# A graph layer on one core: single tiles at the start of the prologue, x in other pieces, the weights' high half on ScalarE

## The chip, the core and the metric

The kernel runs on one core of one Trainium2 chip. The metric is the device time of one execution in microseconds, lower is better. The core has five engines that run their own instruction lists and meet at semaphores: TensorE (PE) for matmuls, VectorE (DVE), ScalarE (ACT), GpSimd (POOL), and the sync engine (SP), which only issues transfers. GpSimd issues transfers too.

## The reference

With N = 2048 nodes and D = 256 features:

```python
h = maximum(layernorm(x), 0)
attn_a = sigmoid(concat([adj @ h, h]) @ Wa.T + ba)      # one gate per node
attn_b = sigmoid(concat([adj @ h, h]) @ Wb.T + bb)
g = h @ W_sa
scores = (g @ a_left)[:, None] + (g @ a_right)[None, :]
e = where(adj != 0, exp(-leaky_relu(scores, 0.01)), 0)
x_a = (e / (sum(e, axis=1) + 1e-5)) @ g
x_b = adj @ (h @ W_gcnb) + b_gcnb
out = x + sigmoid(attn_a * x_a + attn_b * x_b)
```

`adj` is a 2048 x 2048 matrix of zeros and ones. All is fp32; the kernel splits each fp32 operand of a large product into an fp16 high and an fp16 low half (`_hi`, `_lo`) and adds two or three fp16 matmuls.

## The kernel before

The nodes lie in 16 tiles of 128. The output columns of `adj` are taken in four chunks of 512 (`c`). The kernel has a prologue, which works through the 16 tiles of x once, and behind it a long part in which the exponentials of the scores are made and multiplied. The change touches the prologue alone.

The prologue runs over units `u` of two tiles (`NU` = 8). What one unit goes through, with the engine and the line in the kernel before:

- `load_x` (SP, L215): x in five pieces of 2, 2, 4, 4, 4 tiles (`X_PARTS`). The constants `c_sb` and the weights `wa_sb` are issued behind the first piece.
- `moments(u)` (VectorE, L450): for each tile one statistics instruction (L453) and one aggregation of them (L456), and for the unit two small operations (L459, L460) that leave the negated mean and the scaled variance.
- `norms(u)` (GpSimd, L249): the power -0.5 of the variance (L252) and the shift (L254). Between the norms GpSimd issues the pieces of `adj` with `load_adj` (L247), the first when the first piece of x has landed.
- `h0_tiles(u)` (ScalarE, L297): the normalised Relu, in place in `x_sb`, one instruction per tile (L300).
- `turn(u)` (TensorE, L687): transposes of the tile through the identity, two per tile (L693), into bank `u % 2` of PSUM. Unit u waits until unit u - 2 has been read.
- `h0t_highs(u)` (ScalarE, L310) and `h0t_lows(u)` (VectorE, L483): the two fp16 halves of the transposed tiles. Their memory is that of the later `e_hi` and `e_lo`, so the profile names them so.
- `nat_highs(u)` (ScalarE, L306) and `nat_lows(u)` (VectorE, L489): the two halves of the tiles as they are.
- `wide(u)` (TensorE, L704): six matmuls per tile with the weights `wa_hi`, `wa_lo`; 260 columns that hold `g` and four narrow results. Tile t uses one of four banks and waits until tile t - 4 has been read.
- `narrow_results(u)` (VectorE, L494) takes the narrow results out; `mv_highs(u)` (ScalarE, L315 and L319) makes from one of them the exponential scale and the high half of the scaled `g`, one instruction per tile; `mv_lows(u)` (VectorE, L500) the low half.
- `b_products(0, j0, j1)` (TensorE, L730): the aggregation `adj @ h` for chunk 0, four matmuls of 512 columns per tile. It waits for the piece of `adj` and for `nat_lows` of the tile's pair.

No planner sets the order: each engine's list is written out by hand at the end of its block, and each engine goes through its list in that order. In the loop over u, ScalarE does

```python
h0t_highs(u + 1); h0_tiles(u + 2); nat_highs(u + 1); mv_highs(u)
```

and VectorE does

```python
h0t_lows(u + 1); moments(u + 3); narrow_results(u); nat_lows(u + 1); mv_lows(u)
```

so the statistics are three units ahead of the products' halves, and the Relu two. TensorE does `turn(u + 1)`, `wide(u)`, `b_products` of the unit. Before the loop TensorE multiplies zeros (`warm`, L795), nine matmuls (`WARM`) while nothing has landed and six (`WARM_TURN`) between `turn(0)` and `wide(0)`; their results are not used. The product L802 makes four more columns of the wide weights, which VectorE splits in `w_wide` (L463) together with the loaded ones.

Behind the prologue TensorE goes on with `sl_rows`, the aggregation of chunks 1 and 2, and the long products with `e_hi` and `e_lo` (L753 to L755).

Of the kernel before, what the change touches and what calls it, by code (L numbers as in the profile page):

```python
# [67 lines left out]
def build(nc, x, adj_t, w_wide, w_post, consts, rows, out):  # L68
    with ExitStack() as ctx:
# [226 lines left out]
        def _(act):  # L296
            def h0_tiles(u):  # L297
                act.wait_ge(norm_ready, u + 1)
                for t in range(2 * u, 2 * u + 2):
# [8 lines left out]
            def h0t_highs(u):
                act.wait_ge(turned, u + 1)
                act.activation(h0t_hi[:, :, 2 * u * P:(2 * u + 2) * P], turn_bank(u),  # L310
                               ACT.Copy).then_inc(h0t_high, 1)

            def mv_highs(u):
                act.wait_ge(exs_ready, u + 1)
                act.activation(scale_a[:, 2 * u:2 * u + 2], exs[:, 2 * u:2 * u + 2, SR], ACT.Exp, bias=log_s[:, 0:1],  # L315
                               scale=-SLOPE).then_inc(scales_ready, 1)
# [543 lines left out]
```

## Time and profile before

| | us |
|---|---|
| three timed executions | 182.90, 182.56, 182.02 |
| their median | 182.56 |
| the profiled execution | 182.3 |
| its span in the profile | 180.5 |

| engine | busy us | share of the span |
|---|---|---|
| TensorE | 175.3 | 97% |
| VectorE | 146.5 | 81% |
| ScalarE | 115.8 | 64% |
| GpSimd | 17.8 | 10% |

The span is the time from the first to the last instruction; the execution has 1.8 us around it. A high share says which engine has much to do, not when it waits. Where an engine begins to be fed, and by whom, is read from the chain of waits and from the timelines of the first 40 us, which hold the prologue. Starts are in microseconds from the start of the span. Where a row merges several instructions (x2, x9), its length runs from the start of the first to the end of the last; instructions overlap a little at their ends, so the next one of the same engine can start before the one ahead has ended.

### The profile page before, as it was taken

What the parts mean: (1) busy time and instruction counts of PE and PEld (TensorE: products, weight loads), DVE (VectorE), ACT (ScalarE), POOL (GpSimd) and SP (SyncE); (2) the same over time, 40 slices, a digit from 0 to 9 for tenths busy, and PEclk for the clock granted to TensorE, in tenths of its full rate; (3) what the DMA queues carried; (4) which work ended last, traced back from release to release, by engine and by line L of the source; (5) the groups of instructions that cost most, each with busy time, mean ns of one, the idle gap of its engine ahead of it and who ended that gap; (6) DMA issues with size and microseconds to landing.
All of it is one profiled execution on the core that took longest, in us unless ns stands there. A gap on an engine that the chain in (4) does not pass through costs nothing.

```text
span 180.5 us, 3416 instructions
## 1 busy us (share of the span) xinstructions
PE 175.3 (97%) x1335; PEld 128.7 (71%) x1335; DVE 146.5 (81%) x306; ACT 115.8 (64%) x170; POOL 17.8 (10%) x39
## 2 busy tenths in 40 slices
PE   7899999999999999999999999999999999999993
PEld 2656776664544448888864468888888888888892
DVE  1759989748899999599999920999999999987542
ACT  3358788963999987748395640494785686673410
POOL 2544364230000200000000000000000000000000
PEclk9999999999999999999999999999999999999999
DMA  5998967899980598000001100000010010011101
GB/s 172 303 298 143 189 102 162 154 220 241 244 310 5 87 205 172 0 4 0 2 4 58 58 0 4 0 0 0 4 58 0 4 60 0 4 60 56 64 29 29
DMA packets 4767, 15.81 MB, mean 88 GB/s; under 512 B 528, under 2 KB 1040, under 8 KB 3856
## 3 DMA queue, kind: packets, MB, share of 16 engines
q0 software_dynamic: 1440, 8.39, 24.3%
q1 hardware_dynamic: 3312, 7.22, 11.3%
q8 instruction: 10, 0.16, 0.4%
q14 instruction: 5, 0.04, 0.1%
HBM read 21.90 MB, written 2.10 MB: 133 GB/s over the span
## 4 chain that ended last, share of the span: by engine, by line
PE 91%; DMA 7%; DVE 0%; issue 0%; ACT 0%; DVEq 0%
PE ps L730 31%; PE ps L754 16%; PE ps L755 16%; PE ps L753 16%; PE ps L746 6%; PE ps L704 5%; DMA adj<-in_adj_t 5%; DMA x_sb<-in_x 2%; PE ps L693 2%; PE ps L715 1%; DVE logit L673 0%; ACT logit L370 0%; DVE res L589 0%; DVEq L672 0%
## 5 line engine op out<-in xcount | busy, mean ns | idle before, releaser
L753 PE MATMUL ps<-mv_lo,e_hi 128*128 128x257 f16 (+2 forms) x272 | 71.0, 267 | 0.0
L755 PE MATMUL ps<-mv_hi,e_lo 128*128 128x257 f16 (+2 forms) x272 | 70.9, 266 | 0.0
L754 PE MATMUL ps<-mv_hi,e_hi 128*128 128x257 f16 (+2 forms) x272 | 70.8, 266 | 0.0
L336 ACT ACTIVATE z<-z,log_e 128x1024 f32<-128x1024 f32 x32 | 36.7, 1147 | 29.0 <-DVE z L526 29.0
L730 PE MATMUL ps<-adj,nat_hi 128*128 128x512 f16 x128 | 48.5, 379 | 0.2 <-DMA adj<-in_adj_t 0.2
L730 PE MATMUL ps<-adj,nat_lo 128*128 128x512 f16 x128 | 48.5, 379 | 0.0
L526 DVE SCALAR_TENSOR_TENSOR z<-sl_row,exs,far 128x512 f32<-128x512 f32 x64 | 45.1, 746 | 0.0
L534 DVE TENSOR_TENSOR e_lo<-z,e_hi 128x1024 f16<-128x1024 f32 x32 | 39.0, 1219 | 1.3 <-ACT e_hi L346 1.3
L346 ACT ACTIVATE e_hi<-z 128x1024 f16<-128x1024 f32 x32 | 33.3, 1041 | 0.0
L754 PEld LDWEIGHTS ps<-mv_hi,e_hi 128*128 128x128 f16 x272 | 26.5, 98 | 3.2
L753 PEld LDWEIGHTS ps<-mv_lo,e_hi 128*128 128x128 f16 x272 | 26.4, 97 | 3.3
L755 PEld LDWEIGHTS ps<-mv_hi,e_lo 128*128 128x128 f16 x272 | 26.4, 97 | 3.1
L730 PEld LDWEIGHTS ps<-adj,nat_hi 128*128 128x128 f16 x128 | 12.5, 98 | 14.6 <-DMA adj<-in_adj_t 0.5
L730 PEld LDWEIGHTS ps<-adj,nat_lo 128*128 128x128 f16 x128 | 12.5, 98 | 13.9
L515 DVE TENSOR_SCALAR far<-adj 128x1024 f16<-128x1024 f16 x32 | 13.3, 420 | 0.2
L300 ACT ACTIVATE x_sb<-x_sb,shift,rstd 128x256 f32<-128x256 f32 x16 | 8.7, 599 | 4.4 <-POOL shift L254 4.4
L370 ACT ACTIVATE logit<-logit 128x512 f32<-128x512 f32 (+2 forms) x10 | 5.4, 536 | 9.3 <-DVE logit L576 5.3
L543 DVE SCALAR_TENSOR_TENSOR gate_in<-ps,gate_c 128x4 f32<-128x4 f32 x8 | 1.3, 159 | 10.6 <-PE ps L746 10.6
L252 POOL TENSOR_TENSOR rstd<-var_s,power 128x2 f32<-128x2 f32 x8 | 8.1, 1013 | 13.6 <-DVE var_s L460 13.6
L500 DVE SCALAR_TENSOR_TENSOR mv_lo<-ps,scale_a,mv_hi 128x256 f16<-128x256 f32 x16 | 7.0, 480 | 2.5 <-ACT mv_hi L319 2.5
L704 PE MATMUL ps<-wa_hi,e_hi 128*128 128x260 f16 x32 | 8.8, 275 | 0.0
L746 PE MATMUL ps<-wg_hi,agg_hi 128*128 128x258 f16 x32 | 8.8, 274 | 0.0
(69 smaller groups left out, 184.8 us busy)
## 6 DMA issues: line engine op xcount, KB each, us to landing
adj<-in_adj_t POOLq DMA_DIRECT2D x7, 1024.0 KB, 9.7
x_sb<-in_x SPq DMA_DIRECT2D x7, 512.0 KB, 11.4
out<-res SPq DMA_DIRECT2D x7, 256.0 KB, 2.0
x_sb<-in_x SPq DMA_DIRECT2D x2, 256.0 KB, 4.1
adj<-in_adj_t POOLq DMA_DIRECT2D x2, 256.0 KB, 7.1
adj<-in_adj_t POOLq DMA_DIRECT2D x1, 512.0 KB, 5.7
c_sb<-in_consts SPq DMA_DIRECT2D x1, 258.0 KB, 3.5
wa_sb<-in_w_wide SPq DMA_DIRECT2D x1, 258.0 KB, 3.7
```

The lines of the kernel that those rows point to most:

```text
L300: act.activation(x_sb[:, t, :], x_sb[:, t, :], ACT.Relu, bias=shift[:, t:t + 1], scale=rstd[:, t:t + 1]).then_inc(h0_done, 1)
L336: act.activation(z[:, n % ZRING, :, :], z[:, n % ZRING, :, :], ACT.Exp, bias=log_e[:, 0:1], scale=SLOPE - 1.0).then_inc(exp_done, 1)
L346: act.activation(e_hi[:, s:s + 2, :], z[:, n % ZRING, :, :], ACT.Copy).then_inc(e_high, 1)
L515: dve.tensor_scalar(far[:, n % 2, :, :], adj16[:, c % ADJ, j:j + 2, :], -FAR, FAR, ALU.mult, ALU.add)\
L526: ins = dve.scalar_tensor_tensor(out=z[:, n % ZRING, u, :], in0=sl_row[:, c * CW:(c + 1) * CW], scalar=exs[:, j + u, SR:SR + 1], in1=far[: ...
L534: dve.tensor_tensor(e_lo[:, s:s + 2, :], z[:, n % ZRING, :, :], e_hi[:, s:s + 2, :], ALU.subtract)\
L704: ins = pe.matmul(ps[:, WIDE_BANKS[u % 2] + t % 2, 0:WA], h0t[a][:, k, t * P:(t + 1) * P], wa2[b][:, k, :], start=(i == 0), stop=(i == len ...
L730: ins = pe.matmul(ps[:, B_BANKS[c] + k, :], nat[h][:, j, k * P:(k + 1) * P], adj16[:, c % ADJ, j, :], start=(j == 0 and h == 0), stop=(j = ...
L746: ins = pe.matmul(ps[:, 6 + q, 0:WG], agg[a][:, c % AGG, k, cols], wg2[b][:, k, :], start=(i == 0), stop=(i == len(three) - 1))
L753: pe.matmul(ps[:, bank, cols], e_hi[:, s, i1], mv_lo[:, j, cols], start=(j == 0), stop=False)
L754: pe.matmul(ps[:, bank, cols], e_hi[:, s, i1], mv_hi[:, j, cols], start=False, stop=False)
L755: return pe.matmul(ps[:, bank, cols], e_lo[:, s, i1], mv_hi[:, j, cols], start=False, stop=(j == NT - 1))
```

## The change

Units get sizes of their own (`UNITS`): the first four hold one tile each, the other six two tiles, so that `NU` is 10 and the loop begins at unit 4 (`U0`). The Relu, the transposes, the transposed halves, `wide` and the statistics go by units; the natural halves, the narrow results and the scaled `g` still go by pairs of tiles `p`. For unit u of the loop its pair is u - 2. The orders ahead of the loops are written out anew on VectorE, ScalarE and TensorE. x comes in pieces of 1, 1, 2, 4, 4, 4 tiles, the first two ahead of the constants and the weights; SP waits for the piece with tiles 4 to 7 before it issues the last two and what follows them. The high half of the loaded wide weights is made by ScalarE ahead of its first Relu instead of VectorE. `WARM_TURN` is 2 instead of 6. On GpSimd the pieces of `adj` stand between other norms.

The diff without the renaming of u to p in the halves, the narrow results and `mv_highs`, `mv_lows`:

```diff
--- before.py
+++ after.py
@@ -48,17 +48,19 @@
 R_BAB, R_BIAS = 0, 2
 R_END = R_BIAS + D
 
-NU = NT // 2
 WARM = 9
-WARM_TURN = 6
-X_PARTS = ((0, 2), (2, 4), (4, 8), (8, 12), (12, 16))
+WARM_TURN = 2
+UNITS = ((0, 1), (1, 2), (2, 3), (3, 4), (4, 6), (6, 8), (8, 10), (10, 12), (12, 14), (14, 16))
+NU = len(UNITS)
+U0 = 4
+X_PARTS = ((0, 1), (1, 2), (2, 4), (4, 8), (8, 12), (12, 16))
 WIDE_BANKS = (2, 6)
 B_BANKS = (4, 6, 4, 4)
 ADJ_PIECES = ((0, 0, 2), (0, 2, 4), (0, 4, 8), (0, 8, 16), (1, 0, 8), (1, 8, 16), (2, 0, 8), (2, 8, 16), (3, 0, 8), (3, 8, 16))
 
 
 def x_part(u):
-    return next(i for i, (lo, hi) in enumerate(X_PARTS) if lo <= 2 * u < hi)
+    return next(i for i, (lo, hi) in enumerate(X_PARTS) if lo <= UNITS[u][0] < hi)
 
 
 def piece_of(c, j):
@@ -206,7 +209,14 @@
         last_banks = (3, 1)
 
         def turn_bank(u):
-            return ps[:, u % 2, :].rearrange("p (k n) -> p k n", k=KT)
+            n = (UNITS[u][1] - UNITS[u][0]) * P
+            return ps[:, u % 2, 0:KT * n].rearrange("p (k n) -> p k n", k=KT)
+
+        def h0t_cols(tile, u):
+            return tile[:, :, UNITS[u][0] * P:UNITS[u][1] * P]
+
+        def wide_bank(t):
+            return WIDE_BANKS[t // 2 % 2] + t % 2
 
         block = ctx.enter_context(nc.Block())
 
@@ -217,15 +227,18 @@
                 sp.dma_start(x_sb[:, lo:hi, :], x[:, lo:hi, :]).then_inc(x_landed[i], 16)
 
             load_x(0)
+            load_x(1)
             sp.dma_start(c_sb[:, :], consts).then_inc(c_landed, 16)
             sp.dma_start(wa_sb[:, :, :], w_wide).then_inc(wa_landed, 16)
-            load_x(1)
-            for i in range(2, len(X_PARTS)):
-                load_x(i)
+            load_x(2)
+            load_x(3)
+            sp.wait_ge(x_landed[3], 16)
+            load_x(4)
+            load_x(5)
             sp.dma_start(wg_sb[:, :, :], w_post).then_inc(wg_landed, 16)
             sp.dma_start(r_sb[:, :], rows).then_inc(rows_landed, 16)
             sp.wait_ge(turned, NU)
-            sp.wait_ge(nat_ready, NU)
+            sp.wait_ge(nat_ready, NPAIR)
             for g in range(NG):
                 ts = slice(g * GT, (g + 1) * GT)
                 sp.dma_start(x_sb[:, ts, :], x[:, ts, :]).then_inc(x_back[g], 16)
@@ -247,9 +260,9 @@
                 pool.dma_start(adj16[:, c % ADJ, lo:hi, :], adj_t[c, :, lo:hi, :]).then_inc(adj_landed[i], 16)
 
             def norms(u):
-                ts = slice(2 * u, 2 * u + 2)
+                ts = slice(*UNITS[u])
                 pool.wait_ge(var_ready, u + 1)
-                pool.tensor_tensor(rstd[:, ts], var_s[:, ts], power[:, :], ALU.pow).then_inc(rstd_ready, 1)
+                pool.tensor_tensor(rstd[:, ts], var_s[:, ts], power[:, 0:UNITS[u][1] - UNITS[u][0]], ALU.pow).then_inc(rstd_ready, 1)
                 pool.wait_ge(rstd_ready, u + 1)
                 pool.tensor_tensor(shift[:, ts], neg_mean[:, ts], rstd[:, ts], ALU.mult).then_inc(norm_ready, 1)
 
@@ -264,18 +277,20 @@
             norms(1)
             load_adj(1)
             norms(2)
+            norms(3)
             load_adj(2)
-            norms(3)
-            load_adj(3)
             norms(4)
             norms(5)
-            load_adj(4)
+            load_adj(3)
             norms(6)
             norms(7)
+            load_adj(4)
+            norms(8)
+            norms(9)
             load_adj(5)
             load_adj(6)
             load_adj(7)
-            pool.wait_ge(scales_ready, NU)
+            pool.wait_ge(scales_ready, NPAIR)
             pool.tensor_scalar(column[:, :], scale_a[:, :], PROD, None, ALU.mult).then_inc(column_done, 1)
             pool.wait_ge(column_done, 1)
             pool.tensor_copy(mv_hi[:, :, D], column[:, :]).then_inc(column_high, 1)
...
@@ -371,18 +385,32 @@
 
             act.wait_ge(consts_ready, 1)
             act.activation(table[:, :], log_e[:, :], ACT.Exp)
+            act.wait_ge(wa_landed, 16)
+            act.activation(wa_hi[:, :, 0:WG], wa_sb[:, :, :], ACT.Copy, scale=W_SCALE).then_inc(wa_high, 1)
             h0_tiles(0)
             h0t_highs(0)
+            h0_tiles(1)
+            h0t_highs(1)
             nat_highs(0)
-            h0_tiles(1)
-            for u in range(NU):
+            h0_tiles(2)
+            h0t_highs(2)
+            h0_tiles(3)
+            h0t_highs(3)
+            h0_tiles(4)
+            mv_highs(0)
+            nat_highs(1)
+            h0t_highs(4)
+            h0_tiles(5)
+            mv_highs(1)
+            nat_highs(2)
+            for u in range(U0, NU):
                 if u + 1 < NU:
                     h0t_highs(u + 1)
                 if u + 2 < NU:
                     h0_tiles(u + 2)
                 if u + 1 < NU:
-                    nat_highs(u + 1)
-                mv_highs(u)
+                    nat_highs(u - 1)
+                mv_highs(u - 2)
             act.activation(factor_l[:, :], exs[:, :, SL], ACT.Exp, scale=SLOPE).then_inc(factors_done, 1)
             sl_rows(0)
             sl_rows(1)
@@ -448,27 +476,25 @@
             dve.memset(log_s[:, :], math.log(MV_SCALE / PROD)).then_inc(consts_ready, 1)
 
             def moments(u):
+                lo, hi = UNITS[u]
                 dve.wait_ge(x_landed[x_part(u)], 16)
-                for t in range(2 * u, 2 * u + 2):
+                for t in range(lo, hi):
                     dve.bn_stats(stats[:, t, :], x_sb[:, t, :]).then_inc(stats_done, 1)
-                for t in range(2 * u, 2 * u + 2):
+                for t in range(lo, hi):
                     dve.wait_ge(stats_done, t + 1)
                     dve.bn_aggr(mean_var[:, t, :], stats[:, t, :]).then_inc(moments_done, 1)
-                ts = slice(2 * u, 2 * u + 2)
-                dve.wait_ge(moments_done, 2 * u + 2)
-                dve.tensor_scalar(neg_mean[:, ts], mean_var[:, ts, 0], -1.0, None, ALU.mult)
-                dve.tensor_scalar(var_s[:, ts], mean_var[:, ts, 1], LN_EPS, H_SCALE ** -2, ALU.add, ALU.mult)\
+                dve.wait_ge(moments_done, hi)
+                dve.tensor_scalar(neg_mean[:, lo:hi], mean_var[:, lo:hi, 0], -1.0, None, ALU.mult)
+                dve.tensor_scalar(var_s[:, lo:hi], mean_var[:, lo:hi, 1], LN_EPS, H_SCALE ** -2, ALU.add, ALU.mult)\
                     .then_inc(var_ready, 1)
 
-            def w_wide():
-                dve.wait_ge(wa_landed, 16)
-                dve.tensor_scalar(wa_hi[:, :, 0:WG], wa_sb[:, :, :], W_SCALE, None, ALU.mult).then_inc(wa_high, 1)
+            def w_wide_low():
                 dve.wait_ge(wa_high, 1)
                 dve.scalar_tensor_tensor(out=wa_lo[:, :, 0:WG], in0=wa_sb[:, :, :], scalar=W_SCALE, in1=wa_hi[:, :, 0:WG],
                                          op0=ALU.mult, op1=ALU.subtract)
                 dve.wait_ge(wl_product, 1)
-                dve.tensor_scalar(wa_hi[:, :, WG:WA], wl_bank, W_SCALE, None, ALU.mult).then_inc(wa_high, 1)
-                dve.wait_ge(wa_high, 2)
+                dve.tensor_scalar(wa_hi[:, :, WG:WA], wl_bank, W_SCALE, None, ALU.mult).then_inc(wl_high, 1)
+                dve.wait_ge(wl_high, 1)
                 dve.scalar_tensor_tensor(out=wa_lo[:, :, WG:WA], in0=wl_bank, scalar=W_SCALE, in1=wa_hi[:, :, WG:WA],
                                          op0=ALU.mult, op1=ALU.subtract).then_inc(wa_ready, 1)
 
...
@@ -594,20 +618,34 @@
                 logits(p, p)
 
             moments(0)
-            w_wide()
             moments(1)
+            w_wide_low()
             h0t_lows(0)
+            moments(2)
+            h0t_lows(1)
             nat_lows(0)
-            moments(2)
-            for u in range(NU):
+            moments(3)
+            h0t_lows(2)
+            moments(4)
+            narrow_results(0)
+            h0t_lows(3)
+            mv_lows(0)
+            moments(5)
+            nat_lows(1)
+            narrow_results(1)
+            h0t_lows(4)
+            mv_lows(1)
+            moments(6)
+            nat_lows(2)
+            for u in range(U0, NU):
                 if u + 1 < NU:
                     h0t_lows(u + 1)
                 if u + 3 < NU:
                     moments(u + 3)
-                narrow_results(u)
+                narrow_results(u - 2)
                 if u + 1 < NU:
-                    nat_lows(u + 1)
-                mv_lows(u)
+                    nat_lows(u - 1)
+                mv_lows(u - 2)
             w_post_low()
             dve_far(0)
             for n in range(NE):
@@ -687,21 +725,22 @@
             def turn(u):
                 if u >= 2:
                     pe.wait_ge(h0t_ready, u - 1)
-                for t in range(2 * u, 2 * u + 2):
+                for t in range(*UNITS[u]):
                     pe.wait_ge(h0_done, t + 1)
                     for k in range(KT):
-                        ins = pe.transpose(turn_bank(u)[:, k, t % 2 * P:(t % 2 + 1) * P], x_sb[:, t, k * P:(k + 1) * P], ident[:, :])
+                        cols = slice((t - UNITS[u][0]) * P, (t - UNITS[u][0] + 1) * P)
+                        ins = pe.transpose(turn_bank(u)[:, k, cols], x_sb[:, t, k * P:(k + 1) * P], ident[:, :])
                 ins.then_inc(turned, 1)
 
             def wide(u):
                 pe.wait_ge(h0t_ready, u + 1)
                 if u == 0:
                     pe.wait_ge(wa_ready, 1)
-                for t in range(2 * u, 2 * u + 2):
-                    if u >= 2:
+                for t in range(*UNITS[u]):
+                    if t >= 4:
                         pe.wait_ge(mv_ready, t - 3)
                     for i, (k, a, b) in enumerate(three):
-                        ins = pe.matmul(ps[:, WIDE_BANKS[u % 2] + t % 2, 0:WA], h0t[a][:, k, t * P:(t + 1) * P],
+                        ins = pe.matmul(ps[:, wide_bank(t), 0:WA], h0t[a][:, k, t * P:(t + 1) * P],
                                         wa2[b][:, k, :], start=(i == 0), stop=(i == len(three) - 1))
                     ins.then_inc(wide_product, 1)
 
@@ -805,14 +844,22 @@
             pe.wait_ge(ident_ready, 3)
             turn(0)
             warm(WARM_TURN)
+            turn(1)
             wide(0)
-            turn(1)
-            b_products(0, 0, 2)
-            for u in range(1, NU):
+            wide(1)
+            b_products(0, 0, 1)
+            turn(2)
+            b_products(0, 1, 2)
+            wide(2)
+            turn(3)
+            turn(4)
+            wide(3)
+            b_products(0, 2, 4)
+            for u in range(U0, NU):
                 if u + 1 < NU:
                     turn(u + 1)
                 wide(u)
-                b_products(0, 2 * u, 2 * u + 2)
+                b_products(0, *UNITS[u])
             sl_rows(0)
             sl_rows(1)
             b_products(1, 0, 8)
```

## Rows read from the trace of the kernel before

**Rows 1.** The page: busy time of the engines, and the granted clock in 40 slices.

```profile
PE 175.3 (97%) x1335; PEld 128.7 (71%) x1335; DVE 146.5 (81%) x306; ACT 115.8 (64%) x170; POOL 17.8 (10%) x39
...
PEclk9999999999999999999999999999999999999999
```

**Rows 2.** The chain that ended last, 0 to 60 us: start, length, what.

```profile
4.30 8.48 DMA adj<-in_adj_t
...
18.66 1.33 PE ps L704 x12
20.00 1.73 PE ps L730 x8
21.72 0.44 PE ps L693 x4
```

**Rows 3.** Timeline of TensorE: start, length in us, instruction, [idle before it].

```profile
1.18 4.02 PE L795 MATMUL ps<-e_hi 128*128 128x512 f16 x9 [1.18 <-DVE e_hi L446]
...
7.39 1.09 PE L693 MATMUL ps<-ident,x_sb 128*128 128x128 f32 x4 [0.69 <-ACT x_sb L300]
8.27 2.55 PE L795 MATMUL ps<-e_hi 128*128 128x512 f16 x6
10.66 0.27 PE L704 MATMUL ps<-wa_hi,e_hi 128*128 128x260 f16 x1
```

**Rows 4.** Timeline of VectorE.

```profile
4.03 0.75 DVE L453 BATCH_NORM_STATS2 stats<-x_sb 128x6 f32<-128x256 f32 x2 [2.89 <-DMA x_sb<-in_x]
...
13.26 0.69 DVE L483 TENSOR_TENSOR e_lo<-ps,e_hi 128x512 f16<-128x512 f32 x1 [1.68 <-ACT e_hi L310]
13.87 0.74 DVE L453 BATCH_NORM_STATS2 stats<-x_sb 128x6 f32<-128x256 f32 x2
...
17.50 0.74 DVE L453 BATCH_NORM_STATS2 stats<-x_sb 128x6 f32<-128x256 f32 x2
...
18.71 0.68 DVE L489 TENSOR_TENSOR nat_lo<-x_sb,nat_hi 128x512 f16<-128x512 f32 x1
19.67 0.88 DVE L500 SCALAR_TENSOR_TENSOR mv_lo<-ps,scale_a,mv_hi 128x256 f16<-128x256 f32 x2 [0.28 <-ACT mv_hi L319]
20.52 0.69 DVE L483 TENSOR_TENSOR e_lo<-ps,e_hi 128x512 f16<-128x512 f32 x1
```

**Rows 5.** Timeline of ScalarE.

```profile
6.64 1.09 ACT L300 ACTIVATE x_sb<-x_sb,shift,rstd 128x256 f32<-128x256 f32 x2 [4.43 <-POOL shift L254]
8.51 0.60 ACT L310 ACTIVATE e_hi<-ps 128x512 f16<-128x512 f32 x1 [0.78 <-PE ps L693]
...
18.83 0.30 ACT L315 ACTIVATE scale_a<-exs,log_s 128x2 f32<-128x2 f32 x1 [0.48 <-DVE exs L494]
19.16 0.84 ACT L319 ACTIVATE mv_hi<-ps,scale_a 128x256 f16<-128x256 f32 x2
...
20.37 1.09 ACT L300 ACTIVATE x_sb<-x_sb,shift,rstd 128x256 f32<-128x256 f32 x2
21.35 0.63 ACT L306 ACTIVATE nat_hi<-x_sb 128x512 f16<-128x512 f32 x1
```

**Rows 6.** Timeline of GpSimd.

```profile
4.30 0.71 POOL L247 DMA_DIRECT2D adj<-in_adj_t  x1 [2.81 <-DMA x_sb<-in_x]
...
8.33 0.70 POOL L252 TENSOR_TENSOR rstd<-var_s,power 128x2 f32<-128x2 f32 x1 [1.72 <-DVE var_s L460]
...
18.82 1.15 POOL L252 TENSOR_TENSOR rstd<-var_s,power 128x2 f32<-128x2 f32 x1 [1.66 <-DVE var_s L460]
20.05 0.20 POOL L254 TENSOR_TENSOR shift<-neg_mean,rstd 128x2 f32<-128x2 f32 x1
```

**Rows 7.** Timeline of the sync queue.

```profile
1.63 0.42 SPq L221 DMA_DIRECT2D wa_sb<-in_w_wide  x1
```

**Rows 8.** DMA issues by kind: KB each, us from issue to landing.

```profile
wa_sb<-in_w_wide SPq DMA_DIRECT2D x1, 258.0 KB, 3.7
...
out<-res SPq DMA_DIRECT2D x1, 128.0 KB, 1.8
```

More of the change, by code:

```diff
@@ L150, in build @@
         wa_high = sem("wa_high")
+        wl_high = sem("wl_high")
         wa_ready = sem("wa_ready")
@@ L298, in h0_tiles, with nat_highs, mv_highs @@
                 act.wait_ge(norm_ready, u + 1)
-                for t in range(2 * u, 2 * u + 2):
+                for t in range(*UNITS[u]):
                     act.activation(x_sb[:, t, :], x_sb[:, t, :], ACT.Relu, bias=shift[:, t:t + 1],
                                    scale=rstd[:, t:t + 1]).then_inc(h0_done, 1)
-            def nat_highs(u):
-                ts = slice(2 * u, 2 * u + 2)
-                act.wait_ge(h0_done, 2 * u + 2)
-                act.activation(nat_hi[:, ts, :], x_sb[:, ts, :], ACT.Copy).then_inc(nat_high, 1)
             def h0t_highs(u):
                 act.wait_ge(turned, u + 1)
[L310 to L315, printed above, removed]
+                act.activation(h0t_cols(h0t_hi, u), turn_bank(u), ACT.Copy).then_inc(h0t_high, 1)
+            def nat_highs(p):
+                ts = slice(2 * p, 2 * p + 2)
+                act.wait_ge(h0_done, 2 * p + 2)
+                act.activation(nat_hi[:, ts, :], x_sb[:, ts, :], ACT.Copy).then_inc(nat_high, 1)
+            def mv_highs(p):
+                act.wait_ge(exs_ready, p + 1)
+                act.activation(scale_a[:, 2 * p:2 * p + 2], exs[:, 2 * p:2 * p + 2, SR], ACT.Exp, bias=log_s[:, 0:1],
                                scale=-SLOPE).then_inc(scales_ready, 1)
-                act.wait_ge(scales_ready, u + 1)
-                for t in range(2 * u, 2 * u + 2):
-                    act.activation(mv_hi[:, t, 0:D], ps[:, WIDE_BANKS[u % 2] + t % 2, 0:D], ACT.Copy,
+                act.wait_ge(scales_ready, p + 1)
+                for t in range(2 * p, 2 * p + 2):
+                    act.activation(mv_hi[:, t, 0:D], ps[:, wide_bank(t), 0:D], ACT.Copy,
                                    scale=scale_a[:, t:t + 1]).then_inc(mv_high, 1)
@@ L481, in h0t_lows, with nat_lows, narrow_results, mv_lows @@
                 dve.wait_ge(h0t_high, u + 1)
-                cols = slice(2 * u * P, (2 * u + 2) * P)
-                dve.tensor_tensor(h0t_lo[:, :, cols], turn_bank(u), h0t_hi[:, :, cols],
-                                  ALU.subtract).then_inc(h0t_ready, 1)
-            def nat_lows(u):
-                ts = slice(2 * u, 2 * u + 2)
-                dve.wait_ge(nat_high, u + 1)
+                dve.tensor_tensor(h0t_cols(h0t_lo, u), turn_bank(u), h0t_cols(h0t_hi, u), ALU.subtract).then_inc(h0t_ready, 1)
+            def nat_lows(p):
+                ts = slice(2 * p, 2 * p + 2)
+                dve.wait_ge(nat_high, p + 1)
                 dve.tensor_tensor(nat_lo[:, ts, :], x_sb[:, ts, :], nat_hi[:, ts, :], ALU.subtract).then_inc(nat_ready, 1)
-            def narrow_results(u):
-                bank = WIDE_BANKS[u % 2]
-                dve.wait_ge(wide_product, 2 * u + 2)
-                dve.tensor_scalar(exs[:, 2 * u:2 * u + 2, :], ps[:, bank:bank + 2, D:D + NX], 1.0 / PROD, None, ALU.mult)\
+            def narrow_results(p):
+                bank = wide_bank(2 * p)
+                dve.wait_ge(wide_product, 2 * p + 2)
+                dve.tensor_scalar(exs[:, 2 * p:2 * p + 2, :], ps[:, bank:bank + 2, D:D + NX], 1.0 / PROD, None, ALU.mult)\
                     .then_inc(exs_ready, 1)
-            def mv_lows(u):
-                for t in range(2 * u, 2 * u + 2):
+            def mv_lows(p):
+                for t in range(2 * p, 2 * p + 2):
                     dve.wait_ge(mv_high, t + 1)
-                    dve.scalar_tensor_tensor(out=mv_lo[:, t, 0:D], in0=ps[:, WIDE_BANKS[u % 2] + t % 2, 0:D],
+                    dve.scalar_tensor_tensor(out=mv_lo[:, t, 0:D], in0=ps[:, wide_bank(t), 0:D],
                                              scalar=scale_a[:, t:t + 1], in1=mv_hi[:, t, 0:D],
```

4 lines of the change are left out of this document (1 added, 3 removed).

## The prediction

> **What bounds the kernel now.** I read the page first: TensorE is busy 97% of the span, and the page's clock line says full speed everywhere [rows 1]. Then the chain of waits for the first 60 us [rows 2]. Its first long piece is the transfer of the first adjacency piece, which lands at 4.30 + 8.48 = 12.78 us. From there on it is matmuls without a gap: for each pair of tiles 1.33 us of wide projection, 1.73 us of aggregation and 0.44 us of transposes, 3.50 us in all. So the end moves with two things only: when TensorE begins its useful work, and whether it stays fed after that. Third, TensorE's timeline before 11 us [rows 3]: nine matmuls on zeros from 1.18 us, transposes from 7.39 us, six matmuls on zeros from 8.27 us, and the first wide matmul at 10.66 us. Nine 512-column matmuls in 4.02 us, the last one 0.6 us long, start 0.43 us apart; the chain has the same size 1.73/8 = 0.216 us apart at 20 us. So the engine was at its lower level (1.2 GHz) here although the page's clock line shows full speed, and it rose to the upper one (2.4 GHz) shortly before 10.66 us, after some 3 us in which it worked without a pause from 7.39 us.
>
> Last, the timelines of the three engines that feed it [rows 4 to 6]. They are not far from being the bound themselves. VectorE starts the same step (`moments`) at 13.87 and at 17.50 us: a period of 3.63 us against TensorE's 3.50. The cover that makes it work is lookahead: in the loop over units VectorE does `moments(u+3)`, ScalarE `h0_tiles(u+2)`, so that the way from `moments` over GpSimd's `norms` to ScalarE's `h0_tiles` is hidden by a whole pair's work. Each engine takes its instructions in order: at 11.58 us VectorE had all it needed for `moments(3)` (tiles 6 and 7 are in the same x piece as tiles 4 and 5, on which it had just worked), but sat idle 1.68 us until 13.26, because `h0t_lows(1)` stood ahead of it; `moments(3)` began at 13.87 [rows 4].
>
> **The change part by part.**
>
> *x in smaller pieces.* The first piece shrinks from 256 to 128 KB. It now lands at 4.03 [rows 4]; a lone 128 KB transfer takes 1.8 us [rows 8], so the new landing lies between 0.72 + 1.8 = 2.5 and 4.0 us; I take 3.4, a bit nearer to the measured one as others still follow at its heels. `moments(0)` on one tile: statistics 0.41 and the rest as before, about 0.9 us, so done at 4.3 instead of 5.3.
>
> *GpSimd.* `load_adj(0)` moves up with x; the issue is 0.71 us [rows 6] and the power then follows at about 4.4, and `norms(0)` is done at 5.7, `norms(1)` at about 7.
>
> *ScalarE makes the weights' high half first.* The weights land at 1.63 + 3.7 = 5.3 us [rows 7, 8] and are issued one DMA (0.42 us) later now: 5.6. The conversion is like the 512-column `nat_highs`, 0.63 us [rows 5], with 0.51 until the next starts: `h0_tiles(0)` at 6.15 instead of 6.64. It is queued behind the weights, and that eats half of the microsecond just won. VectorE loses the 0.46 us of `wa_hi`.
>
> *Single tiles.* Now ScalarE alternates `h0_tiles` and `h0t_highs` for one tile each. From the end of a Relu to the high half of its transposes it waits 0.78 us (7.73 to 8.51) [rows 5]. A step is 0.49 (half of the pair, 21.35 - 20.37, rows 5) + 0.1 + 0.78 + 0.3 (half of 0.60), near 1.65 us for each of tiles 0 and 1, none of it hidden: tile 0's high half starts at 7.6, tile 1's at 9.3, `nat_highs(0)` at 9.6. VectorE's `nat_lows(0)` follows at 10.3 and is done at 11.0.
>
> *Fewer matmuls on zeros.* Four go, 4 x 0.43 = 1.7 us at the lower level. That removes them from the way to `wide(0)`, which can begin at 9.0, when `h0t_lows(0)` and `turn(1)` are through; so far a gain of 10.66 - 9.0 = 1.7 us. But the engine is then still at its lower level, where a wide tile takes 6 x 0.217 = 1.3 us instead of 0.66: `wide(0)` and `wide(1)` end at 11.2 to 11.6, the aggregation of tile 0 takes 0.86 (upper) to 1.7 us (lower), and `turn(2)` comes behind it: 12.0 to 12.8. The adjacency piece is issued 0.6 us earlier with fewer transfers ahead; bounds from 4.3 to 12.8 us, I take 10.5, not on the path. `h0t_highs(2)` is at 12.4 to 13.2, `h0t_lows(2)` on VectorE at 12.9 to 13.6.
>
> *The new order on VectorE and ScalarE.* Here is the cost. VectorE's list runs: `h0t_lows(2)`, `moments(4)`, `narrow_results(0)`, `h0t_lows(3)`, `mv_lows(0)`, `moments(5)`, `nat_lows(1)`, ..., `mv_lows(1)`, `moments(6)`, `nat_lows(2)`. ScalarE's: `h0_tiles(4)`, `mv_highs(0)`, ..., `h0_tiles(5)`, `mv_highs(1)`. So `mv_lows(0)` waits for `mv_highs(0)`, that is queued behind `h0_tiles(4)`, that needs `moments(4)`; and `moments(5)` is queued behind `mv_lows(0)`. The lookahead is gone: the next pair's statistics begin only when the last pair's whole round has come back. One round, all from rows:
> - `moments` start to power start: 18.82 - 17.50 = 1.32 [rows 4, 6];
> - power start to ScalarE's start: 20.25 - 18.82 = 1.43, + 0.03 = 1.46 [rows 6]; 1.0 if the power is the 0.70 one (it is that short while VectorE is idle, 8.33 us);
> - two Relus: 0.98 [rows 5];
> - the exponential's start to the start of `mv_lows`: 19.67 - 18.83 = 0.84 [rows 4, 5];
> - both `mv_lows`: 20.52 - 19.67 = 0.85 [rows 4].
>
> Sum 5.45 us (5.0 with short powers) where a pair took 3.63. Twice: `moments(4)` starts 0.35 us after `h0t_lows(2)`, at 13.25 to 13.95. `mv_lows(0)` ends 5.45 later, 18.7 to 19.4; `moments(5)` starts there, `mv_lows(1)` ends 24.15 to 24.85; `moments(6)` takes 1.14, and `nat_lows(2)` starts at 25.3 to 26.0 and is done 0.68 later [rows 4], 26.0 to 26.7. TensorE needs it for the aggregation of tiles 4 and 5, which stands on the chain at 20.00 [rows 2]. New: 26.1 to 26.8, middle 26.5. It comes 6.5 us later.
>
> Beyond that point the loop has the old lookahead, TensorE has the same work left in the same order, and nothing of it can be given back, since it runs gapless behind this point and the exponential stage begins on VectorE after the same loop. TensorE's own work up to there is done with waits, so the clock costs little more. The hidden rest: `c_sb` 0.43 us later (its products are small and needed at 9), SP's wait before the last x pieces (tiles 8 on are wanted at 24 us by `moments(6)`, and would be there by 15), the later adjacency pieces (issued behind norms that move with the rest).
>
> Profiled execution: 182.3 = span 180.5 + 1.8 around; + 6.5 gives 188.8. The timed median is 182.56, 0.26 above the profiled one: 189.0.
>
> The Trainium skill, TensorE: Matmul & The Clock Gate, Part 1, says that the array's normal state is throttled and that only activity releases it; the page's advice is not to leave TensorE idle between bursts. The trace shows the release [rows 3], and no fall, as TensorE never pauses afterwards. It is the ground for the second rival.
>
> **The rivals.**
>
> 1. *The start counts and the round is hidden: faster.* Place: TensorE's start. From `turn(1)` at 8.65 it would have 7 x 0.22 of transposes, 6 x 0.665 of wide and 4 x 0.865 of aggregation = 9.0 us until the chain's 20.00, + 1.5 for three microseconds at the lower level: 19.2, 0.8 earlier, 1.5 if the clock rises sooner: 181.4. For it: the first tile is ready sooner, the zeros are gone. Against it: this needs `nat_lows(2)` done by 20.0, and the two rounds would have to take (19.9 - 0.7 - 1.1 - 13.6)/2 = 2.2 us each, where the rows give 5.45. It decides only if the order on the two queues doesn't bind as I read it. 9%.
>
> 2. *The clock falls in the new gaps.* With the rounds, TensorE has some 2.4 us idle before tiles 4 and 5 are turned, as much before the aggregation of tile 2, and about 1.8 before that of tile 4. If it drops to the lower level there, the work behind 26.5 us runs at half speed until it rises again; before, that took 3 us [rows 3], which would cost 1.5 us, more if it comes late: 190.5 to 191.5. For it: it began low and needed work to rise. Against: half of the time it works. 14%.
>
> 3. *Only one round is exposed.* If short powers and quick halves let ScalarE reach `mv_highs(0)` without waiting, one round is as before: 6.5 - 1.8 = 4.7 or, with short powers too, 3.8: 186.4 to 187.3. Against: nothing stands between `moments(4)` and `h0_tiles(4)` that could hide the way. 8%.
>
> 4. *No change*, if late parts have slack that I missed: 3%.
>
> **How the numbers follow.** The forecast (two open rounds) has 66%: 189.0, its own range 187.5 to 190.3 from short powers (-1.0) and the clock rising at 14 instead of 12 us (+0.8). The range reaches into rivals 2 and 3: 186.6 to 191.0. About 0.5% is what a measurement of this kernel can tell from no change. Faster 9%, same 3%, slower 88%.
>
> **What would show it.** In the changed kernel's trace: VectorE idle some 2 us or more before each `mv_lo` of tiles 0 and 2, waiting for ScalarE; ScalarE idle about 2.5 us before the Relu of tiles 6 and 8, waiting for GpSimd's `shift`; the starts of the statistics of tiles 4, 6 and 8 over 5 us apart, then 3.6; aggregation of tiles 4 and 5 near 26 us; first wide matmul near 9 us with 0.22 us between starts. It is wrong if the statistics keep 3.6 us apart from tile 4 on, or if TensorE shows no gaps between 14 and 26 us.

## The result and the profile after

The changed kernel takes 188.74 us (median of four executions, 188.16 to 189.25), the kernel before 182.73 us measured with them. The ratio is 1.0326, 95% interval 1.028 to 1.0371: 6.0 us slower. The profiled execution took 189.25 us, the longest of the four, with a span of 187.4 us: 6.9 more than before. Here and below the ratios leave out executions that are more than 1.5% above the shortest one of their kernel; medians and ranges hold all of them.

The page of the changed kernel, busy time and granted clock:

```profile
PE 177.2 (95%) x1331; PEld 128.8 (69%) x1331; DVE 147.1 (78%) x311; ACT 116.9 (62%) x173; POOL 18.5 (10%) x43
...
PEclk9969579999999999999999999999999999999998
```

TensorE is busy 1.9 us longer for fewer matmuls, and its clock, full in all slices before [rows 1], now is down to 0.5 in places. By stretches of 2 us (busy time and number of PE, PEld, DVE, ACT, POOL, then clock, DMA share, GB/s):

```profile
10.00:12.00 2.00, 2.00 (x11) 1.32 (x9) 1.67 (x6) 0.91 (x2) 0.43 (x3) 0.50 0.89 227
...
18.00:20.00 2.00, 0.69 (x7) 0.37 (x4) 1.74 (x6) 1.60 (x4) 0.00 (x0) 0.80 0.13 25
20.00:22.00 2.00, 0.97 (x3) 0.43 (x4) 1.52 (x6) 0.26 (x1) 1.56 (x3) 0.50 0.01 4
```

A clock of 0.50 is the lower level, 1.2 GHz. The first such stretch is the start. The kernel before is at its lower level at the start too, by the spacing of its matmuls [rows 3], although its clock line reads full. The second is a fall that the kernel before does not have, within 18 to 20 us; TensorE's timeline shows the pauses around it.

```profile
9.16 0.42 PE L743 MATMUL ps<-wa_hi,e_hi 128*128 128x260 f16 x1
9.37 0.43 PE L743 MATMUL ps<-wa_lo,e_hi 128*128 128x260 f16 x1
...
17.19 0.84 PE L732 MATMUL ps<-ident,x_sb 128*128 128x128 f32 x4 [1.89 <-ACT x_sb L315]
17.86 0.27 PE L743 MATMUL ps<-wa_hi,e_hi 128*128 128x260 f16 x1
17.97 0.27 PE L743 MATMUL ps<-wa_lo,e_hi 128*128 128x260 f16 x1
...
21.03 0.58 PE L769 MATMUL ps<-adj,nat_hi 128*128 128x512 f16 x1 [2.33 <-DVE nat_lo L513]
21.41 0.63 PE L769 MATMUL ps<-adj,nat_lo 128*128 128x512 f16 x1
...
26.96 0.38 PE L769 MATMUL ps<-adj,nat_hi 128*128 128x512 f16 x1
```

The first wide matmul starts at 9.16 us (10.66 before, rows 3), the second 0.21 us later: lower level. A pause of 1.89 us follows; behind it the wide matmuls are still 0.11 us apart, the upper level. Then a pause of 2.33 us, and behind that 512-column matmuls of 0.63 us, 0.42 us apart: the lower level. The Trainium skill (TensorE: Matmul & The Clock Gate, Part 1) has an idle engine go back to the lower level. The trace agrees as far as that: the granted clock is 0.80 over 18 to 20 us, in which the second pause begins, and 0.50 from 20 us on. The aggregation of tiles 4 and 5 starts at 26.96. The chain of waits:

```profile
2.10 4.03 DMA wa_sb<-in_w_wide
...
16.45 1.09 ACT x_sb L315 x2
...
18.26 0.88 DVE mv_lo L524 x2
...
21.03 3.57 PE ps L769 x8
24.60 0.85 PE ps L732 x4
25.45 1.67 PE ps L743 x12
27.12 1.73 PE ps L769 x8
```

Before, the chain was matmuls alone from 12.8 us [rows 2]; now it goes through Relus, `mv_lo` and statistics. And from 21.03 to 27.12 us it is TensorE's own work for tiles 2 and 3, their followers' transposes and the wide tiles 4 and 5: 6.1 us of what took 3.5 (1.73 + 0.44 + 1.33, rows 2). The piece of 1.73 us on tiles 4 and 5, the landmark for what follows, is at 27.12 instead of 20.00: 7.1 us later. (The chain gives a piece from the end of the one ahead of it, so it can stand 0.16 us behind the start in the timeline.) The feeding engines, VectorE first, then ScalarE:

```profile
14.10 0.74 DVE L482 BATCH_NORM_STATS2 stats<-x_sb 128x6 f32<-128x256 f32 x2
...
18.26 0.88 DVE L524 SCALAR_TENSOR_TENSOR mv_lo<-ps,scale_a,mv_hi 128x256 f16<-128x256 f32 x2 [2.08 <-ACT mv_hi L333]
19.05 0.74 DVE L482 BATCH_NORM_STATS2 stats<-x_sb 128x6 f32<-128x256 f32 x2
...
23.56 0.88 DVE L524 SCALAR_TENSOR_TENSOR mv_lo<-ps,scale_a,mv_hi 128x256 f16<-128x256 f32 x2 [2.00 <-ACT mv_hi L333]
24.35 0.74 DVE L482 BATCH_NORM_STATS2 stats<-x_sb 128x6 f32<-128x256 f32 x2
...
25.49 0.68 DVE L513 TENSOR_TENSOR nat_lo<-x_sb,nat_hi 128x512 f16<-128x512 f32 x1
```

```profile
16.45 1.09 ACT L315 ACTIVATE x_sb<-x_sb,shift,rstd 128x256 f32<-128x256 f32 x2 [0.72 <-POOL shift L267]
...
21.74 1.09 ACT L315 ACTIVATE x_sb<-x_sb,shift,rstd 128x256 f32<-128x256 f32 x2 [2.14 <-POOL shift L267]
```

Statistics start at 14.10, 19.05 and 24.35 us: rounds of 4.95 and 5.30 us where the kernel before has 3.63 [rows 4]. Ahead of each `mv_lo` VectorE is idle 2 us for ScalarE, which was idle 2.14 us for the shift of tiles 6 and 7. `nat_lo` of tiles 4 and 5 is done at 25.49 + 0.68 = 26.2 us, 0.8 us before TensorE reaches them. So two limits lie side by side there: the open rounds (26.2) and TensorE's own work at the lower level (27.0). They are not independent: the pause in which the clock fell, and the start of that work at 21.03, are themselves waits for the first open round.

### The profile page after: what moved, and what is told of

It is laid out like the page before. It is cut to its first block, busy times and chain, and to the rows that moved or that the text cites. A ratio compares the mean times of both kernels' runs of the same rounds, so it can differ in the third digit from the quotient of the medians.

```text
span 187.4 us, 3423 instructions
## 1 busy us (share of the span) xinstructions
PE 177.2 (95%) x1331; PEld 128.8 (69%) x1331; DVE 147.1 (78%) x311; ACT 116.9 (62%) x173; POOL 18.5 (10%) x43
## 4 chain that ended last, share of the span: by engine, by line
PE 90%; DVE 3%; ACT 2%; DMA 2%; SPq 1%; issue 1%; POOL 0%; DVEq 0%
PE ps L769 30%; PE ps L794 15%; PE ps L793 15%; PE ps L792 15%; PE ps L743 6%; PE ps L785 6%; DMA wa_sb<-in_w_wide 2%; PE ps L732 2%; ACT x_sb L315 1%; PE ps L754 1%; DVE stats L482 1%; DVE mv_lo L524 0%; SPq L227 0%; ACT e_hi L320 0%; POOL rstd L265 0%
## 5 line engine op out<-in xcount | busy, mean ns | idle before, releaser
L769 PE MATMUL ps<-adj,nat_hi 128*128 128x512 f16 x128 | 49.7, 388 | 2.3 <-DVE nat_lo L513 2.3
L769 PE MATMUL ps<-adj,nat_lo 128*128 128x512 f16 x128 | 49.6, 388 | 0.0
L769 PEld LDWEIGHTS ps<-adj,nat_hi 128*128 128x128 f16 x128 | 12.8, 100 | 17.1 <-issue 3.7
L265 POOL TENSOR_TENSOR rstd<-var_s,power 128x2 f32<-128x2 f32 (+1 forms) x10 | 8.1, 809 | 19.5 <-DVE var_s L488 19.4
L743 PE MATMUL ps<-wa_hi,e_hi 128*128 128x260 f16 x32 | 9.6, 300 | 0.1
L743 PE MATMUL ps<-wa_hi,e_lo 128*128 128x260 f16 x32 | 9.5, 297 | 0.0
```

Source lines behind the costliest of these rows:

```text
L743: ins = pe.matmul(ps[:, wide_bank(t), 0:WA], h0t[a][:, k, t * P:(t + 1) * P], wa2[b][:, k, :], start=(i == 0), stop=(i == len(three) - 1))
L769: ins = pe.matmul(ps[:, B_BANKS[c] + k, :], nat[h][:, j, k * P:(k + 1) * P], adj16[:, c % ADJ, j, :], start=(j == 0 and h == 0), stop=(j = ...
```

## The experiments

**stats_ahead.** The changed kernel, with the statistics one place ahead on VectorE:

```diff
             moments(3)
+            moments(4)
             h0t_lows(2)
-            moments(4)
+            moments(5)
             narrow_results(0)
             h0t_lows(3)
             mv_lows(0)
-            moments(5)
+            moments(6)
             nat_lows(1)
             narrow_results(1)
             h0t_lows(4)
             mv_lows(1)
-            moments(6)
             nat_lows(2)
```

> The changed kernel with one edit on VectorE: moments(4), moments(5) and moments(6) each move one place ahead, in front of h0t_lows(2), narrow_results(0) and nat_lows(1), so that the statistics of a pair no longer wait for mv_lows of the pair before. ScalarE's and TensorE's lists stay. Theory (the open rounds cost the time): the Relus of tiles 6 and 8 no longer wait over 1 us for GpSimd, the starts of mv_lo of tiles 0 and 2 are under 4 us apart instead of 5.3, and some 3 of the 6 to 7 us come back: 185.5, 184.8 to 186.5. What is left is the late start of tiles 2 and 3, whose nat_lows(1) still stands behind moments(6) and mv_highs(0). Rival (single tiles and fewer matmuls on zeros cost it, the order doesn't matter): 188 to 189, as the changed kernel.

Measured: 187.16 us, 185.58 to 188.69; over the three shorter ones of the four the ratio is 1.0225 (1.0167 to 1.0282). The rounds closed; VectorE and then the chain of the profiled execution, which is the longest of the four and not among those three:

```profile
17.28 0.88 DVE L524 SCALAR_TENSOR_TENSOR mv_lo<-ps,scale_a,mv_hi 128x256 f16<-128x256 f32 x2 [1.25 <-ACT mv_hi L333]
...
20.84 0.88 DVE L524 SCALAR_TENSOR_TENSOR mv_lo<-ps,scale_a,mv_hi 128x256 f16<-128x256 f32 x2 [0.27 <-ACT mv_hi L333]
```

```profile
20.05 3.57 PE ps L769 x8
23.62 0.85 PE ps L732 x4
24.47 2.10 PE ps L743 x12
26.57 1.73 PE ps L769 x8
```

`mv_lo` of tiles 0 and 2 are 3.56 us apart (5.30 in the changed kernel), as expected. Of the expected 3.2 us 1.8 came back (by the ratios). In the profiled execution TensorE's own work from tiles 2 and 3 to tiles 4 and 5 takes 6.5 us, nearly all of it at the lower level, and it alone binds. My expectation had no term for the clock, and that was wrong there. The other three are 0.9 to 3.1 us shorter, with a mean granted clock of 0.991 against 0.971; no trace shows what binds them.

**zeros_in_gaps.** The changed kernel, TensorE kept busy:

```diff
             turn(3)
+            spare(7, 8)
             turn(4)
             wide(3)
+            spare(1, 10)
             b_products(0, 2, 4)
```

`spare(bank, n)` multiplies zeros, n matmuls of 512 columns, into a free bank; for bank 1 it first waits until the transposes there have been read.

> The changed kernel with matmuls on zeros in TensorE's two gaps: 8 of 512 columns between turn(3) and turn(4), 10 between wide(3) and the aggregation of tiles 2 and 3, into banks that nobody reads then. Theory (the clock fell in the gaps and cost TensorE the last 0.8 us): the spacing of the 512-column matmuls on tiles 2 and 3 is 0.22 us instead of 0.43, and the aggregation of tiles 4 and 5 then waits for nat_lows(2) alone, at 26.2 instead of 26.96 us: 0.8 us faster than the changed kernel, 187.9 against 188.7. Rival (the clock cost much more than the waits, so that the open rounds explain only part): 3 us or more faster. Second rival (the clock had no effect on the end): no change, within 0.3 us.

Measured: 188.18 us, ratio 1.0303 (1.0268 to 1.0339); by time alone not told apart from the changed kernel. The chain says what binds:

```profile
25.09 0.60 DVE nat_lo L513
...
25.83 1.89 PE ps L769 x8
```

The granted clock is 1.00 from 12 us on, and TensorE waits for `nat_lo` of tiles 4 and 5, which starts at 25.09: the other limit, as expected. It starts on tiles 4 and 5 at 25.83, 1.1 us ahead of the changed kernel's 26.96. Of this 0.4 us is not the edit's: the weights landed at 5.64 us here (6.13 in the changed kernel), and `nat_lo` too started 0.4 us earlier. The 0.7 us left are the 0.8 that I expected.

**ahead_and_zeros.** Both edits (4 and 10 zeros).

> Both edits at once: the statistics of tiles 4 to 9 one place ahead on VectorE (as in stats_ahead) and matmuls on zeros in TensorE's gaps (4 and 10). Each alone gave little: with the statistics ahead the profiled execution had TensorE at its lower level from 19 to 25.8 us, so that tiles 2 and 3 to tiles 4 and 5 took 6.4 us of its own work instead of 3.5; with zeros alone it waited for nat_lows(2) until 25.8 us. Theory (two limits side by side, the open round on VectorE and ScalarE, and TensorE's clock behind the gaps): together they bring the aggregation of tiles 4 and 5 from 26.96 to about 20.05 + 3.5 = 23.6 us: 3.4 us off the changed kernel, 185.3 (184.7 to 185.9), with less spread than stats_ahead alone. Rival (the effects only add up): 188.7 - 1.6 - 0.6 = 186.5 or more.

Measured: 185.5 us, 184.98 to 186.92, ratio 1.0168 (1.0127 to 1.0209).

```profile
18.46 0.60 DVE nat_lo L513
...
19.20 1.89 PE ps L769 x8
...
22.86 1.73 PE ps L769 x8
```

Tiles 4 and 5 at 22.86 us. By their ratios, times 182.6 us, the four kernels stand at +6.0 (neither edit), +5.5 (zeros), +4.1 (statistics ahead) and +3.1 us (both) over the kernel before. So the pair takes back 2.9 us where the single edits add up to 2.3, which the intervals do not tell from a sum: the times do not decide between my theory and its rival. In the chains the landmark is at 27.12, 25.83, 26.57 and 22.86, 4.3 us for the pair against 1.8 for the single edits. But these are one execution each, for neither edit and for the statistics alone the longest of its kernel, for the pair the shortest. That there are two limits is read from the chains, each with one of them binding; how much they overlap in a usual execution is not shown. What is left is the late start of tiles 2 and 3: their `nat_lo` at 18.46, behind `mv_lows(0)` and `moments(6)`.

**before_one_late.** The kernel before, one line moved:

```diff
             nat_lows(0)
-            moments(2)
             for u in range(NU):
                 if u + 1 < NU:
                     h0t_lows(u + 1)
+                if u == 0:
+                    moments(2)
```

> The kernel before with one edit on VectorE: moments(2) no longer stands ahead of the loop but behind h0t_lows(1), right before moments(3). No single tiles, no new pieces of x, all the matmuls on zeros. Theory: this alone opens one round, from the statistics of tiles 4 and 5 over GpSimd to the Relu, that mv_highs(0) stands behind. In the kernel before the statistics start at 10.35 us; now at 13.9, the Relu at 16.6 instead of 13.12, mv_lows(0) at about 18.9 instead of 16.04. VectorE and ScalarE come 2.9 us later, of which TensorE's cover at the end of the prologue takes 0.3: 2.6 us slower, 185.2; up to 186.2 if the clock falls in the new gap. Rival (lookahead is worth little, since TensorE has other work): within 0.7 us of the kernel before.

Measured: 186.53 us (186.43 to 186.71), ratio 1.0223 (1.0201 to 1.0245): 3.9 us for one line, with none of the change's other parts. ScalarE, then the chain:

```profile
16.25 1.09 ACT L300 ACTIVATE x_sb<-x_sb,shift,rstd 128x256 f32<-128x256 f32 x2 [2.98 <-POOL shift L254]
```

```profile
18.08 2.60 PE ps L705 x12
...
24.31 1.73 PE ps L731 x8
```

The exposed way is there (2.98 us idle for the shift), and the wide tiles 2 and 3 took 2.60 us instead of 1.33. I had 2.6 us, or 3.6 with a fall of the clock; it fell, and 3.9 is a little above both.

**one_late_and_zeros.** The same with `warm(9)` in the gap, behind the aggregation of tiles 0 and 1.

> The kernel before with moments(2) behind h0t_lows(1) (as in before_one_late, 3.9 us slower than before) and nine matmuls on zeros behind the aggregation of tiles 0 and 1, in the 2 us gap that this opens. Theory: 2.6 us of the 3.9 are the exposed way from the statistics to the Relu, 1.3 us are the wide projection of tiles 2 and 3 at the lower level; with the clock kept up, 185.3. Rival (the gap itself is the price, the clock adds nothing): 186.5, no change against before_one_late.

Measured: 185.05 us (184.32 to 185.15), ratio 1.012 (1.0081 to 1.0159).

```profile
14.99 1.94 PE ps L796 x9
...
17.37 1.33 PE ps L705 x12
18.70 1.73 PE ps L731 x8
```

The wide tiles take 1.33 us again. What is left over the kernel before, 2.2 to 2.5 us (by the ratio, by the medians), is the exposed round; the 1.5 to 1.9 us that went were the clock.

**relu_first.** The changed kernel, ScalarE's first two steps swapped:

```diff
+            h0_tiles(0)
             act.wait_ge(wa_landed, 16)
             act.activation(wa_hi[:, :, 0:WG], wa_sb[:, :, :], ACT.Copy, scale=W_SCALE).then_inc(wa_high, 1)
-            h0_tiles(0)
```

> The changed kernel with one edit on ScalarE: the Relu of tile 0 stands ahead of the high half of the weights. Theory (the chain of the changed kernel begins with the transfer of the weights, which ScalarE waits for until 6.15 us while the shift of tile 0 is there at 5.28): the first Relu at 5.3, tile 0's transposes done before the weights are split, its high half at 6.7 instead of 7.87, about 0.6 to 1.1 us earlier for all that follows until the adjacency piece or the norms bind: 187.9, 0.8 faster. Rival (the gain is lost at norms(2) or at the first adjacency piece): no change.

Measured: 188.54 us, ratio 1.0327 (1.0274 to 1.0379): no change, the rival.

```profile
3.47 7.89 DMA adj<-in_adj_t
...
20.38 3.57 PE ps L769 x8
...
26.72 1.73 PE ps L769 x8
```

The chain now begins with the first adjacency piece, which lands at 11.36 us; of the 0.8 us 0.4 arrive at tiles 4 and 5, too little to measure.

**before_two_zeros.** The kernel before with `WARM_TURN = 2`.

> The kernel before with WARM_TURN 2 instead of 6 and nothing else. Theory (the aggregation of tiles 0 and 1 waits for the first adjacency piece until 12.8 us anyway): wide(0) starts at about 9.9 us instead of 10.7 and ends before 12.8 us even at the lower level; no change, within 0.4 us of 182.6. Rival (the zeros are what brings the clock up in time): TensorE still at the lower level at 12.8 us, up to 1.5 us slower.

Measured: 183.11 us, ratio 1.0021 (1.0003 to 1.0039). 0.4 us by the ratio, 0.5 by the medians: at the edge of what I gave. In the kernel before, four zeros fewer do not cost the 6 us. In the profiled execution the adjacency piece landed at 13.66 us; TensorE was up in time although `wide(0)` ran at the lower level.

```profile
4.17 9.48 DMA adj<-in_adj_t
```

**three_lists.** All parts of the change, with the lookahead restored. The lists up to the loops, w for the weights' halves:

```
VectorE: moments 0, 1, w low, h0t_lows 0, moments 2, h0t_lows 1, moments 3, nat_lows 0,
  moments 4, h0t_lows 2, nat_lows 1, moments 5, narrow 0, moments 6, h0t_lows 3,
  mv_lows 0, h0t_lows 4, narrow 1, nat_lows 2, mv_lows 1
ScalarE: h0_tiles 0, w high, h0t_highs 0, h0_tiles 1, h0t_highs 1, nat_highs 0,
  h0_tiles 2, 3, h0t_highs 2, nat_highs 1, h0_tiles 4, h0t_highs 3, mv_highs 0,
  h0t_highs 4, h0_tiles 5, nat_highs 2, mv_highs 1
TensorE: turn 0, zeros x2, turn 1, wide 0, 1, turn 2, b 0, 1, turn 3, wide 2, turn 4,
  b 2, 3, wide 3
```

> All parts of the change kept, with all three lists written anew so that the lookahead is back: VectorE does moments(3) ahead of nat_lows(0), moments(4) ahead of h0t_lows(2), nat_lows(1), moments(5), narrow_results(0), moments(6), h0t_lows(3), mv_lows(0), h0t_lows(4), narrow_results(1), nat_lows(2), mv_lows(1); ScalarE does the Relu of tile 0 ahead of the weights, the Relus of tiles 2 and 3 together, nat_highs(1) ahead of h0_tiles(4), nat_highs(2) ahead of mv_highs(1); TensorE turns tile 2 ahead of the aggregation of tile 0 and tile 3 ahead of wide(2). Theory (the order was the price; single tiles and the earlier start are worth about a microsecond once it is paid): from the durations in the rows, VectorE is busy nearly without a gap from 8 us and TensorE from 8.4 us; the prologue's last aggregation ends at 38.1 instead of 38.96 us: 181.8 (181.2 to 182.8), faster than both. Rival (single tiles themselves are too dear, by ScalarE's round trip per tile and the extra instructions): 183.5 or more.

Measured: seven of its twelve executions took 181.7 to 182.6 us, five took 185 to 188. The ratio over the seven is 0.996 (0.9935 to 0.9986); the median of all twelve is 182.42 us. VectorE and the chain of one of the five:

```profile
19.05 0.75 DVE L482 BATCH_NORM_STATS2 stats<-x_sb 128x6 f32<-128x256 f32 x2 [4.33 <-DMA x_sb<-in_x]
```

```profile
3.04 8.26 DMA x_sb<-in_x
...
11.32 7.71 DMA x_sb<-in_x
...
23.01 2.60 PE ps L743 x12
```

SP waits for the piece with tiles 4 to 7 before it issues the next; here that piece landed at 11.30 and the next at 19.02, and VectorE stood 4.33 us. TensorE's clock fell in the gap that this made, so that the 12 wide matmuls behind it took 2.60 us instead of 1.33. SP's wait did not bind in the changed kernel, whose `moments(6)` came at 24.35; with the tight order it costs up to 6 us in five executions of twelve.

**lists_x_no_wait, lists_x_wait_2, lists_stats6_later.** three_lists, with SP's wait taken out; with the wait on the piece with tiles 2 and 3; and that with `moments(6)` behind `h0t_lows(4)`.

```diff
-            sp.wait_ge(x_landed[3], 16)
+            sp.wait_ge(x_landed[2], 16)
```

> three_lists without SP's wait for the piece with tiles 4 to 7: all x pieces are issued at once, as in the kernel before. In three_lists 7 of 12 executions took 181.7 to 182.6 us and 5 took 185 to 188; in a profiled one of the latter the piece with tiles 8 to 11 was issued only at 11.3 us, when its forerunner had landed, and landed at 19.0, beside the adjacency pieces; moments(6) waited 4.3 us for it, with mv_lows(0) queued behind it on VectorE. Theory (the wait on SP makes the slow executions): none above 183.5 now. The first adjacency piece has more ahead of it and lands near 12.8 as in the kernel before instead of 11.5, which costs up to 1 us: 182.3 (181.6 to 182.9). Rival (the slow executions have another cause, the clock): they stay.

> three_lists with SP's wait on the piece with tiles 2 and 3 instead of that with tiles 4 to 7: the last x pieces are issued at about 7 us instead of 9.3 to 11.3. Theory: they land at 11 to 14 us, in time for moments(6) at 14.5; the median stays at 181.8 and the executions above 184 go. The adjacency piece lands between 11.4 and 12.8. 181.9 (181.4 to 182.6).

> lists_x_wait_2 with moments(6) behind h0t_lows(4) on VectorE instead of ahead of h0t_lows(3), so that a late x piece blocks less. Theory: moments(6) is still early enough for the Relu of tiles 8 and 9, at the price of at most 0.5 us of lookahead: 182.2, no execution above 184 even if the piece is late. Rival (it reopens the round for tiles 8 and 9): 183.5 or more.

| | median us | executions | ratio to before | 95% interval |
|---|---|---|---|---|
| lists_x_no_wait | 181.88 | 181.14 to 183.86 | 0.9957 | 0.9933 to 0.9981 |
| lists_x_wait_2 | 181.80 | 180.87 to 181.92 | 0.9935 | 0.9912 to 0.9959 |
| lists_stats6_later | 181.55 | 181.32 to 182.52 | 0.9951 | 0.9931 to 0.9971 |

The executions of 185 us and more, five of three_lists' twelve, are gone: none in the 27 of these three (one of no_wait took 183.86, just above the bound I gave, and is not in its ratio). three_lists was measured on another chip and not again beside them. The three are not told apart; by the ratios they are 0.8 to 1.2 us faster than the kernel before. The chain of lists_x_wait_2:

```profile
11.35 1.89 PE ps L769 x8
...
15.08 1.73 PE ps L769 x8
...
19.73 1.73 PE ps L769 x8
```

Tiles 4 and 5 stand at 19.73 us, before at 20.00.

## Why the prediction was right

**The start.** Right within 0.6 us, with misses that cancel. The forecast stands in brackets. x landed at 3.41 (3.4). The power of a single tile took 0.59 us, where the first one of the kernel before, for two tiles, takes 0.97, so the shift of tile 0 was there at 5.28, not 5.7; it didn't matter, since the weights landed at 6.13 instead of 5.6 us and ScalarE makes their high half first. Tile 0's high half was at 7.87 (7.6), tile 1's at 9.40 (9.3), `wide(0)` at 9.16 (9.0), at the lower level as forecast.

**The rounds.** Right, and the largest term: `moments(4)` at 14.10 (13.25 to 13.95), rounds of 4.95 and 5.30 us (5.0 to 5.45), `nat_lows(2)` done at 26.2 (26.0 to 26.7). Of the signs one is weaker than forecast: ScalarE waited 2.14 us for the shift of tiles 6 and 7, but 0.97 for that of tiles 8 and 9, where I had about 2.5 for both. before_one_late shows the mechanism alone, stats_ahead that moving three lines closes the rounds. three_lists shows that the order was the price: all the other parts of the change are in it, and seven of its twelve executions are no slower than the kernel before; with SP's wait moved or gone, all three kernels are faster. It changes the lists of three engines at once, TensorE's too, so it does not show how much of the 6 us each list holds; moving VectorE's three lines alone gave back 1.8.

**The clock.** The weak step. "TensorE's own work up to there is done with waits, so the clock costs little more": in the profiled execution TensorE took 5.9 us from 21.03 to 26.96 us for 3.5 us of work, and it bound at the last, by 0.8 us. The second rival took place, but I had put its price behind the rounds, as an addition of 1.5 us or more; in the profiled execution it lies beside them and adds 0.8. That the total fitted all the same (6.5 forecast, 6.0 by the medians, 6.9 in the profile) is in part luck: the two limits happened to end 0.8 us apart, and nothing in the prediction said that they would. It may also be why the first repair gave 1.8 us instead of 3.2, but that is shown only for the profiled execution of stats_ahead.

**The range.** The two terms that the prediction names for its own range, -1.0 and +0.8 us, give 188.0 to 189.8; the 0.5 us more on either side have no term. The measured 188.74 lies within either.

**The rival "faster".** Its condition, rounds of 2.2 us, was not met. Its size, 0.8 to 1.5 us by the earlier start, is what the reordered kernels reach (0.8 to 1.2); no run takes apart where they gain it.

**Said to be hidden.** SP's wait: hidden in the changed kernel, not in a tight one.

## What to carry to other kernels

Engines that take their lists in order need the long way round (statistics, power, Relu) issued one stage ahead of the work that waits for it; when a prologue is written anew, follow one item from each producer round to the place in its list where its successor stands, and add up that loop: if it is longer than the bound engine's period, it is the new period. Look for the clock in every gap that a new order opens on TensorE: the work behind the gap can become a second limit beside the wait that made the gap, and then repairing the one leaves the other. A transfer held back by a wait should be tried again once the order around it is tighter.

## What the runs showed that I had not expected

The granted clock of a stretch can read 1.00 while TensorE is at its lower level. The page's line of the kernel before had hinted at it [rows 1, 3]; the clock by stretches does it too, and not always: over 10 to 12 us the changed kernel reads 0.50 with its 260-column matmuls 0.2 us apart, and before_two_zeros, at the same spacing, reads 1.00. In before_two_zeros (start, length; clock of the stretch in the third column from the end):

```profile
9.79 0.40 PE L704 MATMUL ps<-wa_hi,e_hi 128*128 128x260 f16 x1 [0.56 <-DVE e_lo L483]
9.98 0.42 PE L704 MATMUL ps<-wa_lo,e_hi 128*128 128x260 f16 x1
```

```profile
10.00:12.00 2.00, 2.00 (x11) 1.42 (x10) 1.45 (x7) 0.50 (x2) 0.43 (x1) 1.00 1.06 288
```

The 260-column matmuls start 0.2 us apart, half the rate of the 0.11 us [rows 2], beside a clock of 1.00. Read the spacing too, above all in the first 12 us.
